# Part of a shared expert's work moved between the attention and the expert stage of a gated block with a mixture of experts

## The chip, the cores and the metric

The kernel is one launch on one core of a Trainium2 chip. The metric is the device time of that launch in microseconds (us). Five engines work side by side and meet only at semaphores: TensorE (PE, with PEld for its weight loads), VectorE (DVE), ScalarE (ACT), GpSimd (POOL) and SyncE (SP), which here only issues DMA transfers. Each engine runs its own instructions strictly in the order in which they are written, so an instruction that waits holds back all that stands behind it on that engine.

## What is computed

Sixteen batches of 128 tokens with 512 features go through cross attention and then through a mixture of experts; each part adds to its input through a gate.

```python
x = x + tanh(g_xattn) * attention(layernorm(x), ctx, pos, pos, Wq, Wkv, Wout, bout)   # 32 heads of 16, rotary
x = x + tanh(g_ffn)   * ffn(layernorm(x))

def ffn(x):                                     # 2048 tokens
    shared_out = silu_and_mul(x @ shared_w1.T) @ shared_w2.T       # inner width 704
    probs = softmax(x @ gate_w.T)                                   # 16 experts
    weights, selected = top_k(probs, 6)
    # each expert: silu_and_mul(x @ w1[e].T) @ w2[e].T, inner width 352, weighted, summed over the 6
    return moe_out + shared_out
```

All of it is float32; the large products are made from a high and a low part of each operand (x_hi, x_lo and w_hi, w_lo), three matmuls for one product.

## The kernel before

**Stage A, attention (`phase_a`).** A pipeline of five stages runs over the 16 batches: LOAD, PROJECT, ATTEND, TAIL, PLACE. In round r, stage k works on batch r - k, so there are 20 rounds: six written out, a loop, and four written out in which the stages run dry (rounds 16 to 19). A round has eight steps, u = 0 to 7. LOAD takes the statistics of the input (L868) and, at u = 7, scales it into `xn` (L875); PROJECT transposes `xn` on PE at u = 0 (L629) and makes q, k and v (L622), with POOL doing the rotary pairs (L429, L431); ATTEND makes scores (L647), their maxima on DVE (L902) and exponentials on ACT (L529); TAIL projects out (L734), adds the residual (L947), and scales it into `row` (L909) after POOL has made a reciprocal root by Newton steps (L436 to L447); PLACE transposes `row`, computes the gate, picks six experts for each token, and scatters the rows into an array in HBM sorted by expert (`expert_rows`, L459, POOL). On DVE, at u = 7, the order is `place`, then `row`, then `xn`. At the end of round 19 `block_table` builds on DVE a table that says for each block of 128 sorted rows which expert it belongs to; it is stored and loaded back by SP.

**Weights of the experts.** POOL splits each expert's weights into high and low parts (`split_w1` L205 and L209, `split_w2` L217 and L220) and loads the next ones (`load_after_split`). There are two places in SBUF (`SLOTS`), so the split of the weights after next waits until the expert that holds the place is done. The first two experts are split inside stage A, at the end of rounds 2 to 5 (`early_weights`): `split_w1` in rounds 2 and 4, `split_w2` in rounds 3 and 5.

**Between the stages** a block ends and another begins: all engines meet, then SP waits for the table, for all scattered rows and for the first padding rows, and only then loads the first rows of stage B.

**Stage B, experts (`phase_b`).** 143 steps: 111 steps (`BLOCKS`) of one routed block each, and then 32 for the shared expert, which is cut into two halves of width 352, two steps for each batch. Step i on PE is `down` of step i - 2 (L1413, 9 matmuls), `transpose_act` of step i - 1 (L1390, 3), `up` of step i (L1379, 24). On DVE a step turns the next tile (L1449), makes its low part `x_lo` (L1454), makes `a_lo` of step i - 1 (L1458) and `gated` of step i (L1470). SP loads each tile in four quarters (L1200) and the weights of its tokens (L1212), writes padding rows (L1191, L1192) during the first steps, and stores y.

**The end.** For each batch POOL gathers six rows of y for each token (L1301, six indirect DMAs). DVE adds them in `combine_rows` (L1477, 1536 elements wide) and `combine` (L1483 to L1486), and `finish` (L1493) adds the shared expert's result. The steps at which this happens are in `sum_at` and `finish_at`: one batch every two steps. POOL's two buffers let the gather of batch b start when `combine_rows` of batch b - 2 is done. The lines that set the order on DVE there:

```python
            if i is not None and i in finish_at and i != STEPS: finish(...)
            if starts_tile(i, 1): turn_x, meta, x_low
            if live(i, -1): a_low(*at(-1))
            if live(i, 0): gated(i, at)
            if i in sum_at: combine(sum_at[i])
            if i + 1 in sum_at: combine_rows(sum_at[i + 1])
```

## Time and profile before

| what | value |
|---|---|
| median of 3 runs | 1453.27 us (1451.62 to 1455.07) |
| the profiled execution | 1454.81 us, span 1452.9 us, mean granted PE clock 0.962 |
| PE busy | 1338.6 us, 92% of the span, 8414 matmuls |
| DVE, ACT, POOL busy | 764.0, 562.6, 698.3 us |
| PE's share of the chain that ended last | 74% |

The profile is of one execution. Times in it are counted from the first instruction; an engine's line number is that of the listing above. "Idle before" is the time in which the engine stood still just ahead of an instruction, with what released it. The granted clock is 1.0 at 2.4 GHz and 0.5 at 1.2 GHz.

### The profile page before, as it was taken

Reading aid. Unit: us, or ns where it says so; the run is one execution under the profiler, and the core shown is the slowest. Engines: PE = TensorE matmul, PEld = TensorE weight load, DVE = VectorE, ACT = ScalarE, POOL = GpSimd, SP = SyncE. Lnnn points to the kernel's source line nnn. Section 1 sums busy time; section 2 is a strip of 40 time slices with the busy share of each in tenths; the row PEclk is TensorE's granted clock in tenths of the full one; section 3 lists DMA queues with packets and bytes.
Section 4 is the critical chain, followed back from the end, with each engine's and each line's share of the span. In section 5 each row is a group of like instructions: output and inputs, shape, how many; then the busy total and the mean of one; then the engine's idle time right before and its main releaser. Section 6 shows DMA issues by size and latency. Waiting matters only on the chain.

```text
span 1452.9 us, 32739 instructions
## 1 busy us (share of the span) xinstructions
PE 1338.6 (92%) x8414; PEld 1144.2 (79%) x8415; DVE 764.0 (53%) x1554; ACT 562.6 (39%) x1366; POOL 698.3 (48%) x1135
## 2 busy tenths in 40 slices
PE   4897899989988639999999999999999999999998
PEld 2565666666666438999999999999999999898997
DVE  4467557667666443444444444444444443356666
ACT  3565566666666212333333333333233332211111
POOL 3556655555554333286554454545345500745553
PEclk8899899999999659999999999999999999999999
...
GB/s 194 30 93 79 138 98 134 77 89 142 77 103 102 81 186 142 140 148 148 119 141 108 148 148 143 145 140 148 148 145 143 113 115 88 117 161 213 196 206 145
DMA packets 146858, 190.04 MB, mean 131 GB/s; under 512 B 32531, under 2 KB 99604, under 8 KB 144116
## 3 DMA queue, kind: packets, MB, share of 16 engines
...
## 4 chain that ended last, share of the span: by engine, by line
PE 74%; DVE 7%; POOL 6%; issue 5%; ACT 4%; SPq 2%; POOLq 0%; DMA 0%; DVEq 0%; ACTq 0%
PE bank L1379 35%; PE bank L1413 19%; PE bank L622 4%; PE bank L629 3%; PE bank L1390 3%; PE bank L647 3%; PE bank L734 2%; ACT soft L529 2%; PE bank L661 2%; PE bank L678 1%; POOL w_lo L209 1%; DVE smax L902 1%; POOL newt L445 1%; DVE x L947 1%; POOL expert_rows L459 1%
## 5 line engine op out<-in xcount | busy, mean ns | idle before, releaser
L1379 PE MATMUL bank<-w_hi,x_hi 128*128 (+1 forms) x1144 | 289.2, 334 | 20.2 <-DVE x_lo L1454 18.2
L1379 PE MATMUL bank<-w_hi,x_lo 128*128 (+1 forms) x1144 | 276.9, 323 | 0.0
L1379 PE MATMUL bank<-w_lo,x_hi 128*128 (+1 forms) x1144 | 276.7, 323 | 0.0
L205 POOL CAST w_hi<-w_raw 128x352 fp32r<-128x352 f32 x144 | 69.0, 527 | 379.1 <-PE bank L1379 379.1
L1470 DVE SCALAR_TENSOR_TENSOR act<-silu,row_w,bank 128x352 f32<-128x352 f32 x111 | 64.4, 580 | 299.9 <-ACT silu L1328 299.4
L1328 ACT ACTIVATE silu<-bank 128x352 f32<-128x352 f32 x143 | 66.4, 464 | 400.8 <-PE bank L1379 400.8
L1379 PEld LDWEIGHTS bank<-w_hi,x_hi 128*128 128x128 f32 x1144 | 192.7, 189 | 20.7 <-issue 18.3
L1379 PEld LDWEIGHTS bank<-w_lo,x_hi 128*128 128x128 f32 x1144 | 199.8, 189 | 0.0
L1379 PEld LDWEIGHTS bank<-w_hi,x_lo 128*128 128x128 f32 x1144 | 199.3, 189 | 0.0
L1413 PE MATMUL bank<-w_hi,a_hi 128*128 (+3 forms) x429 | 171.4, 400 | 7.3 <-DVE a_lo L1458 7.0
L529 ACT ACTIVATE soft<-bank,smax 128x128 f32<-128x128 f32 x512 | 146.8, 379 | 80.1 <-DVE smax L902 80.1
L1317 ACT ACTIVATE x_hi<-x_t 128x512 fp32r<-128x512 f32 x127 | 80.2, 632 | 234.2 <-DVE x_t L1449 234.2
L1413 PE MATMUL bank<-w_hi,a_lo 128*128 (+3 forms) x429 | 169.7, 396 | 0.0
L1413 PE MATMUL bank<-w_lo,a_hi 128*128 (+3 forms) x429 | 169.5, 395 | 0.0
L1301 POOL DMA_INDIRECT gath<-y_rows,y_slots x96 | 96.9, 1010 | 90.7 <-DVE tree L1477 60.7
L209 POOL TENSOR_TENSOR w_lo<-w_raw,w_hi 128x352 fp32r<-128x352 f32 x144 | 137.5, 985 | 0.0
L1454 DVE TENSOR_TENSOR x_lo<-x_t,x_hi 128x512 fp32r<-128x512 f32 x127 | 113.7, 895 | 35.0 <-ACT x_hi L1317 29.8
L459 POOL DMA_INDIRECT expert_rows<-row,slots x96 | 94.7, 986 | 35.5 <-issue 33.1
L1449 DVE STREAM_TRANSPOSE x_t<-xr 128x512 f32<-128x512 f32 x127 | 89.8, 707 | 21.3 <-DMA xr<-expert_rows 21.0
L902 DVE TENSOR_REDUCE smax<-bank 128x4 f32<-128x512 f32 x128 | 84.8, 683 | 29.7 <-PE bank L647 28.7
L1413 PEld LDWEIGHTS bank<-w_hi,a_hi 128*128 128x128 f32 (+1 forms) x429 | 80.7, 188 | 23.7 <-DVE a_lo L1458 7.2
L1413 PEld LDWEIGHTS bank<-w_hi,a_lo 128*128 128x128 f32 (+1 forms) x429 | 80.9, 188 | 19.3
...
## 6 DMA issues: line engine op xcount, KB each, us to landing
...
y_rows<-y SPq DMA_DIRECT2D x111, 256.0 KB, 2.1
...
```

The lines of the kernel that those rows point to most:

```text
L205: nc.gpsimd.tensor_copy(w1_hi[d][half][:, s], w1_raw[:, d, halves[half]]).then_inc(w_hi_made, 1)
L209: nc.gpsimd.tensor_tensor(w1_lo[d][half][:, s], w1_raw[:, d, halves[half]], w1_hi[d][half][:, s].bitcast(F32), ALU.subtract).then_inc(w1_m ...
L459: g.indirect_dma_start(rows, bass.IndirectOffsetOnAxis(slots[j][:, k:k + 1], 0), row[j][:], None)\
L529: last = a.activation(soft[u % 2][:, h, :], bank[2 + u % 2][:, h * P:(h + 1) * P], ACT.Exp, bias=smax[u % 2][:, h:h + 1])
L902: v.tensor_reduce(smax[u % 2][:], s3, AX.X, ALU.max, negate=True).then_inc(smax_done, 1)
L1301: nc.gpsimd.indirect_dma_start(gath[b % 2][:, k, :], None, y_rows, bass.IndirectOffsetOnAxis(y_slots[:, b * 8 + k:b * 8 + k + 1], 0))\
L1317: a.activation(x_hi[j][:], x_t[:], ACT.Copy).then_inc(x_hi_done, 1)
L1328: a.activation(silu[j][:], g_bank[:, 0:WIDTH], ACT.Silu).then_inc(silu_done, 1)
L1379: last = nc.tensor.matmul(to[:, 0:WIDTH], xx[jt][:, d, :], w[d][half][:, cols], start=(d == 0 and xx is x_hi and w is w1_hi), stop=(d == D ...
L1413: last = nc.tensor.matmul(to[:], l[j][0:m, c, :], w[c][0:m, cols], start=(first and c == 0 and k == 0), stop=(final and c == 2 and k == 2))
L1449: v.transpose(x_t[:].rearrange("p c (i t) -> p i c t", i=4), xr[j][:].rearrange("p (i c e) -> p i c e", i=4, c=DC)).then_inc(x_turned, 1)
L1454: v.tensor_tensor(x_lo[j][:], x_t[:], x_hi[j][:].bitcast(F32), ALU.subtract).then_inc(x_lo_done, 1)
```

## The change

- **Half of the shared expert for batches 0 to 5 comes first.** Six steps (`EARLY = 6`) of its first half are numbered 0 to 5, the routed blocks are steps 6 to 116, and the shared expert's other 26 half steps follow. The number of steps stays 143. The result of an early step is added to x1 on DVE (`add_early`) and stored over x1 in HBM.
- **No block boundary.** Both stages' programs stand in one block. Early steps 0, 1 and 2 are laid by hand into rounds 17 to 19: their loads on SP, `turn_x` and `x_low` on DVE, `x_high` and `gate` on ACT, and on PE a quarter of `up` in each of u = 0 to 3 of round 18, the whole of step 1's at u = 6, and so on. Steps 3 to 5 follow `block_table`, and parts of the early steps stand between the links of that table's chain on DVE. SP waits for the table at step 3.
- **Weight splits.** The shared expert's first half is place 0, split in rounds 1 to 3 (half of `split_w1` in round 1, half in round 2, `split_w2` in round 3). The first routed expert's weights are split in rounds 17 and 18. The shared first half is loaded and split once more at the end, so there are 19 places (`PLACES`) for 18.
- **The input's scaling ahead of the row.** On DVE at u = 7, `xn` now stands ahead of `place` and `row`.
- **Order at the end.** `sum_at` puts a batch on every 1.4 steps from the fourth shared step on; on DVE the sums stand between `a_low` and `gated`; the first gather stands ahead of the last `split_w2`; five PSUM banks hold y for three.

The diff below is cut. Its pieces are, in order: the constants, POOL's splits in the early rounds, POOL's last rounds, PE's last rounds, DVE's round at u = 7, SP in stage B, POOL's last place, the steps of the sums, and DVE in a step of stage B.

```diff
+EARLY = 6
+ROUTED_END = EARLY + BLOCKS
+TILES = ROUTED_END + BATCHES
+PLACES = [EXPERTS, *range(EXPERTS), EXPERTS + 1, EXPERTS]
...
                     if r == 0:
                     pool.wait_ge(w_hi_done, 1)
                     load_w(nc.gpsimd, 0)
-                if r in (2, 4):
-                    split_w1(pool, r // 4)
-                if r in (3, 5):
-                    split_w2(pool, r // 4)
-                    load_after_split(pool, r // 4 + 1)
+                if r == 1:
+                    split_w1(pool, 0, range(0, 2))
+                if r == 2:
+                    split_w1(pool, 0, range(2, 4))
+                if r == 3:
+                    split_w2(pool, 0)
+                    load_after_split(pool, 1)
...
+                if last_round(at, ATTEND):
+                    pool.wait_ge(v_mm, BATCHES)
+                    clear_act()
+                    split_w1(pool, 1)
+                if last_round(at, TAIL):
+                    split_w2(pool, 1)
+                    load_after_split(pool, 2)
...
+                    if last_round(at, TAIL) and u < 4:
+                        up_part(0, u)
...
+                    if last_round(at, TAIL):
+                        if u == 4:
+                            transpose_act(0, 0, 0)
+                        if u == 6:
+                            for d in range(DC):
+                                up_part(1, d)
+                    if last_round(at, PLACE):
+                        if u == 0:
+                            down_part(2, 0)
+                            down_part(2, 1)
+                        if u == 1:
+                            down_part(2, 2)
+                            transpose_act(1, 1, 0)
+                            up_part(2, 0)
+                            up_part(2, 1)
+                        if u == 6:
+                            up_part(2, 2)
...
+                    if at(LOAD) and u == 7:
+                        load(u, *at(LOAD))
                     if at(PLACE) and u == 7:
                         place(*at(PLACE))
...
-                    if at(LOAD) and u == 7:
-                        load(u, *at(LOAD))
...
             def one_step(i, at):
+                if i == EARLY - 3:
+                    rows_complete()
...
+                    if place + 1 == len(PLACES):
+                        pool.wait_ge(slot_chain, 2 * EXPERTS - 1)
+                        for j in range(2):
+                            pool.wait_ge(y_out[j], 16 * (EARLY // 2 + (BLOCKS + 1 - j) // 2))
+                        gather(0)
...
+        sum_at = {ROUTED_END + 4 + math.ceil(1.4 * b): b for b in range(BATCHES)}
+        finish_at = {max(last_step[ROUTED_END + b] + 2, step + 1): b for step, b in sum_at.items()}
...
+                if shared and i - 1 in sum_at and sum_at[i - 1] < BATCHES - 1:
+                    combine(sum_at[i - 1])
+                if shared and i in sum_at:
+                    combine_rows(sum_at[i])
+                if shared and i in finish_at:
                     finish(finish_at[i])
                 if live(i, 0):
                     gated(i, at)
-                if i is not None and i in sum_at:
-                    combine(sum_at[i])
-                if i is not None and i + 1 in sum_at:
-                    combine_rows(sum_at[i + 1])
+                if i == STEPS - 1:
+                    combine(BATCHES - 1)
```

**Place 1: DVE at the end of a full round of stage A** (u = 6 and 7). Before, from the last two maxima of the scores to the input's scaling:

```order
L902 TENSOR_REDUCE smax<-bank 128x4 x2
L997 TENSOR_TENSOR slot_e<-bank,const 128x16
L999 TENSOR_TENSOR seen<-seen,mask 128x16
L1001 TENSOR_TENSOR pick_slot<-pick,slot_e 128x96
L1004 TENSOR_REDUCE slot_f<-pick_slot 128x6
L1007 CAST slots<-slot_f 128x8
L1008 COPY slots_all<-slot_f 128x8
L909 TENSOR_SCALAR row<-x,mean,rstd 128x4x4x32
L875 TENSOR_SCALAR xn<-x_sb,mean,rstd 128x512
```

After, the same stretch:

```order
L1009 TENSOR_REDUCE smax<-bank 128x4 x2
L982 TENSOR_SCALAR xn<-x_sb,mean,rstd 128x512
L1104 TENSOR_TENSOR slot_e<-bank,const 128x16
L1106 TENSOR_TENSOR seen<-seen,mask 128x16
L1108 TENSOR_TENSOR pick_slot<-pick,slot_e 128x96
L1111 TENSOR_REDUCE slot_f<-pick_slot 128x6
L1114 CAST slots<-slot_f 128x8
L1115 COPY slots_all<-slot_f 128x8
L1016 TENSOR_SCALAR row<-x,mean,rstd 128x4x4x32
```

`xn` has moved from behind `row` to ahead of the placing.

**Place 2: PE in round 18,** the last TAIL round, from the last values of attention (`soft_t`) on. Before, the attention's last transposes and the output projection (`at_hi`) follow at once:

```order
L678 MATMUL bank<-soft_t,v_one 17x128 x4
L629 MATMUL bank<-const,ot 128x128 x4
L629 MATMUL bank<-const,attn 128x128 x4
L734 MATMUL bank<-w_hi,at_hi 128x512
L734 MATMUL bank<-w_lo,at_hi 128x512
```

After (L1553 is `up` of the early step 0, a quarter at a time):

```order
L765 MATMUL bank<-soft_t,v_one 17x128 x4
L1553 MATMUL bank<-w_hi_0,x_hi 128x352
L1553 MATMUL bank<-w_hi_1,x_hi 128x352
L1553 MATMUL bank<-w_lo_0,x_hi 128x352
L1553 MATMUL bank<-w_lo_1,x_hi 128x352
L1553 MATMUL bank<-w_hi_0,x_lo 128x352
L1553 MATMUL bank<-w_hi_1,x_lo 128x352
L716 MATMUL bank<-const,ot 128x128 x4
```

Six expert matmuls have come in ahead of each of these waits.

**Place 3: DVE in the shared steps at the end.** Before, two steps of a pair:

```order
L1470 SCALAR_TENSOR_TENSOR act<-silu,tanh,bank 128x352
L1483 TENSOR_TENSOR tree<-tree 128x512
L1484 TENSOR_TENSOR tree<-tree,x_t 128x512
L1486 TENSOR_TENSOR comb<-tree 128x512
L1477 TENSOR_TENSOR tree<-gath 128x1536
L1493 TENSOR_TENSOR o_t<-bank,comb 128x512
L1458 TENSOR_TENSOR a_lo<-bank,a_hi 128x384
L1470 SCALAR_TENSOR_TENSOR act<-silu,tanh,bank 128x352
```

After, the seventh step behind the routed blocks, in which all three kinds of sum fall together:

```order
L1652 TENSOR_TENSOR a_lo<-bank,a_hi 128x384
L1648 TENSOR_TENSOR x_lo<-x_t,x_hi 128x512
L1682 TENSOR_TENSOR tree<-tree 128x512
L1683 TENSOR_TENSOR tree<-tree,x_t 128x512
L1685 TENSOR_TENSOR comb<-tree 128x512
L1676 TENSOR_TENSOR tree<-gath 128x1536
L1692 TENSOR_TENSOR o_t<-bank,comb 128x512
L1669 SCALAR_TENSOR_TENSOR act<-silu,tanh,bank 128x352
```

The sums have moved from behind `act` and ahead of `a_lo` to behind `a_lo` and ahead of `act`.

## Rows read from the trace of the kernel before

**Rows 1.** The page's 40 slices of the span, tenths busy and granted clock.

```profile
PE   4897899989988639999999999999999999999998
PEclk8899899999999659999999999999999999999999
```

**Rows 2.** Busy us (instructions) by stretch: PE, PEld, DVE, ACT, POOL; clock, DMA share, GB/s.

```profile
115.53:149.95 34.42, 26.63 (x205) 19.29 (x205) 24.33 (x50) 18.28 (x52) 25.17 (x51) 0.90 0.23 83
149.95:185.45 35.50, 29.23 (x205) 20.90 (x205) 19.61 (x50) 18.40 (x52) 21.82 (x44) 0.86 0.39 141
270.00:297.23 27.23, 25.13 (x206) 17.99 (x205) 18.64 (x50) 18.38 (x52) 14.45 (x35) 1.00 0.29 103
457.96:482.66 24.70, 19.28 (x168) 12.92 (x169) 14.67 (x41) 15.97 (x48) 8.82 (x21) 0.94 0.28 99
482.66:516.86 34.20, 18.80 (x78) 14.20 (x78) 13.26 (x52) 3.57 (x9) 14.76 (x25) 0.55 0.30 118
516.86:535.01 18.15, 0.00 (x0) 0.00 (x1) 6.92 (x30) 0.63 (x1) 7.02 (x9) 0.50 0.54 177
535.01:576.22 41.21, 37.59 (x196) 34.01 (x197) 15.05 (x28) 11.34 (x21) 10.17 (x15) 0.92 0.52 164
576.22:1232.86 656.64, 656.64 (x3781) 608.88 (x3781) 296.81 (x524) 205.98 (x421) 298.60 (x392) 1.00 0.45 135
1249.21:1447.36 198.15, 193.29 (x1093) 176.81 (x1092) 118.52 (x169) 36.91 (x76) 97.03 (x97) 1.00 0.63 184
```

**Rows 3.** Who waited for whom from 60 to 470: us in total, times, longest.

```profile
PE bank L629 <- DVE xn L875: 12.9, 13, 1.2
PE bank L629 <- POOL q_cos L431: 11.4, 2, 7.1
```

**Rows 4.** POOL by time in stage A: start, us, [idle before].

```profile
44.55 0.85 POOL L429 TENSOR_TENSOR q_cos<-q_cos,q_sin 128x256 f32<-128x256 f32 x1 [15.39 <-DVE q_sin L861]
...
125.99 7.12 POOL L209 TENSOR_TENSOR w_lo<-w_raw,w_hi 128x352 fp32r<-128x352 f32 x8
...
478.44 0.19 POOL L436 TENSOR_SCALAR neg_half<-mean 128x1 f32<-128x1 f32 x1 [12.26 <-DVE mean L952]
```

**Rows 5.** DVE at the end of round 15: start, us, [idle before].

```profile
432.28 0.55 DVE L909 TENSOR_SCALAR row<-x,mean,rstd 128x512 f32<-128x512 f32 x1 [2.38 <-POOL rstd L447]
432.74 0.54 DVE L875 TENSOR_SCALAR xn<-x_sb,mean,rstd 128x512 f32<-128x512 f32 x1
```

**Rows 6.** DVE from the last count to the first tile of stage B.

```profile
517.10 0.17 DVE L1022 TENSOR_TENSOR pad_at<-cnt,const 128x16 int32<-128x16 f32 x1
...
522.87 0.15 DVE L1055 TENSOR_SCALAR table_p<-tb 128x1 int32<-128x1 f32 x1
532.78 0.71 DVE L1449 STREAM_TRANSPOSE x_t<-xr 128x512 f32<-128x512 f32 x1 [9.76 <-DMA xr<-expert_rows]
```

**Rows 7.** PE by time: the first matmuls of `up` of step 112.

```profile
1243.56 0.59 PE L1379 MATMUL bank<-w_hi,x_hi 128*128 128x352 f32 x2 [2.04 <-POOL w_lo L209]
```

**Rows 8.** DVE in a shared step: the sums and what stands behind them.

```profile
1412.58 0.69 DVE L1486 TENSOR_TENSOR comb<-tree 128x512 f32<-128x512 f32 x1
1413.38 1.76 DVE L1477 TENSOR_TENSOR tree<-gath 128x1536 f32<-128x1536 f32 x1
1415.06 0.68 DVE L1493 TENSOR_TENSOR o_t<-bank,comb 128x512 f32<-128x512 f32 x1
```

**Rows 9.** All gathers: POOL's time for one issue, and to landing.

```profile
L1301 POOL DMA_INDIRECT gath<-y_rows,y_slots x96: 940/946/2291, 1249.5 to 1434.7; - x96
...
DMA to landing us min/median/max: 3.2/3.9/6.4
```

**Rows 10.** DVE beside POOL's splits: x_lo's ns min/median/max over 127, and one `prob`.

```profile
L1454 DVE TENSOR_TENSOR x_lo<-x_t,x_hi x127: 691/693/4192, 534.2 to 1428.9; 128x512 fp32r<-128x512 f32 x127
...
129.06 4.87 DVE L975 TENSOR_SCALAR prob<-gexp,grec 128x16 f32<-128x16 f32 x1
```

**Rows 11.** ACT's change from exponential to silu.

```profile
537.22 1.28 ACT L1328 ACT_TABLE_LOAD   x1
```

514 lines of the change are left out of this document (330 added, 184 removed).

## The prediction

> **What bounds the kernel now.** I read the page's slices first [rows 1]: PE is at nine tenths or more nearly everywhere, with one deep hole in slices 13 and 14, the hand-over from attention to experts, where its clock is also granted at half. So PE's order of work bounds the kernel, and gains can only come from places where PE stands still or runs at 1.2 GHz. The table by stretch gives these places their size [rows 2]. From 576.22 to 1232.86 PE does 105 routed steps without a gap: 656.64 / 105 = 6.25 us a step. I use that as the price of a step. A full attention round takes 27.23 us, of which PE is busy 25.1. Two early rounds take 34.42 and 35.50. From 457.96, where round 17 begins, to 576.22, where the sixth expert step's `up` has ended, 118.3 us pass. At the end 198.15 us hold 30 steps and the start of the last.
>
> The change leaves the number of expert steps at 143 and adds no matmul. I therefore sum what PE loses before and after in four places.
>
> **1. The weight splits in early rounds.** The two long rounds lose 34.42 + 35.50 - 2 x 27.23 = 15.5 us [rows 2]. PE waits 11.4 us of that, in two waits, the longest 7.1, for POOL's rotary pairs [rows 3]; POOL was in the splits behind a scatter, `w_lo` alone 7.12 us [rows 4]. The rest fits the granted clock, 0.90 and 0.86 in those rounds against 1.00 [rows 2]. After the change no split stands in rounds 4 and 5. Round 1 gets half a `split_w1`, about 5 us, where POOL idled 15.39 us [rows 4]; round 2 gets the other half where the whole was, round 3 keeps its `split_w2`. What hides them is that idle; without it they would cost what they cost now. I take **-15.5**; bounds -11.4 (only the waits go) and -18 (a remainder of low clock in the round after goes too).
>
> **2. `xn` ahead of `row`.** PE waited 12.9 us in 13 rounds for `xn` [rows 3], about 1 us each. On DVE `row` ended at 432.83, having waited for POOL's root, and `xn` only began at 432.74 [rows 5]. After, `xn` is made while DVE would idle (2.38 us before `row`), so it is hidden; PE has its 0.5 us of transposes to do and then meets the next wait, for `row`, which is ready at 432.88 against 432.78. About 0.1 of the 1.0 us stays, and DVE's next maximum moves forward by the 0.46 that `xn` took, not by 1.0. I take 0.8 for each of 13 rounds, **-10.5**; bounds 0 (the round closes on POOL's root and takes up the whole gain) and -13.
>
> **3. The hand-over.** Before: 118.3 us. After, in PE's order, with DVE and ACT followed along:
> - Round 17: 24.7 as before [rows 2], plus the tiles of the early steps on DVE (four operations of 0.7) of which perhaps half are hidden, plus their collisions with `split_w1`, which now stands on POOL ahead of the last-but-one root. That root idled 12.26 us [rows 4] and the split with its clearing takes 11.5, so POOL itself is just in time. I take 26.2.
> - From there to the end of `up` of step 5, PE has: attention's rest in rounds 18 and 19, about 9.7 us at full clock (18.80 us busy before at 0.55 [rows 2]); six `up`, four `down`, five transposes, 33.2 us. Sum 42.9. Waits: about 0.6 for the output projection, 1.8 for the last `row` (POOL's root is 3.7 us and only `up` of step 1 covers the chain from o to row), 0.3 small ones.
> - Step 6 needs the table and its rows. DVE's table chain took 5.8 us from the count [rows 6] and now also carries `gated`, `x_low`, `a_low` and `add_early`, 2.5 us and a short wait, so it ends about 9 us after the count. From its end to the first tile turned took 9.9 us before (522.87 to 532.78 [rows 6]); SP now has more padding rows ahead of it, and issues a store and an x1 load first. Set against steps 3 to 5, 18.7 us of PE work, tile 6 comes about 3 us late, and DVE stands before it with `a_low` and `gated` queued behind. I take 3.0.
> - The clock. Before, it fell near 480 and stayed at half for the hole (0.55, 0.50 [rows 2]). Step 112 shows what a short gap costs: a wait of 2.04 us [rows 7], then an `up` from 1243.56 to 1249.21, 5.65 us, where a step's 6.25 less `down` and transposes (2.43) leaves 3.82, so 1.8. I take that three times, once for round 18 and once behind each wait: 5.5 in all.
>
> After: 26.2 + 42.9 + 2.7 + 3.0 + 5.5 = 80.3; with 1.6 for what I can't see in a hand-made order, 81.9. **-36.4**; bounds -26 (round 18 at half clock all through, and a blocked DVE) and -43 (no loss of clock).
>
> **4. The end.** Before: `up` of step 112 waits 2 us for the last split and is 1.8 us long [rows 7]. 30 steps and the last `down`'s wait would be 30 x 6.25 + 3.5 = 191.0, and took 198.15 [rows 2], since `combine` and `combine_rows` stand ahead of `a_lo` in DVE's queue: 7.1. Together 10.9. After: the shared half that comes first is split while expert 15 runs, and the other one is needed six steps later, so the 3.8 goes. The sums now stand ahead of `act`. In a step with all three, `a_lo` ends 3.5 us after the step begins, then 0.6 (x_low) + 2.1 + 1.7 + 0.6 + 0.6 (act) (the sums by [rows 8]): 9.1, and PE wants `act` at 8.35 (one step and one `down`). Nine of the 26 steps have `combine` and `combine_rows` together. Four of them also make a tile: 0.75 late each; five do not: 0.15 each. That is 3.8, and the last `combine` now stands ahead of the last `a_lo`: 1.3. Together 5.1, so **-5.8**. The gathers: six issues of 0.95 with 0.3 between them are 7.5 us for each batch, and one every 8.75 us fits. Where two sums are only two steps apart there are 12.8 us for 7.5 + 3.9 to landing [rows 9], 1.1 to spare; at the longest landing, 6.4, three gathers are 1.4 late, and act with them. Bounds: +20 (below) and -9.
>
> **Sum.** 1454.8 (this execution) - 15.5 - 10.5 - 36.4 - 5.8 = 1386.6. The median of the three runs is 1.5 below this execution, so **1385**.
>
> **A rule against the change.** POOL's split in round 17 now runs beside DVE. In the profile `x_lo` takes 693 ns at the median and 4192 at the longest, and `prob` once took 4.87 us beside a split [rows 10]. The Trainium skill (SBUF — State Buffer, Who interferes with whom) says that a DVE instruction with two SBUF inputs, or in a two-port mode, and a GpSimd one that reads SBUF lock each other out for the whole instruction. By that rule each of about three such operations waits for one POOL instruction at most, under 1 us, and my 1.5 us for round 17 holds. The two long rows are longer than one POOL instruction, so the trace disagrees for them. By the rows, `prob` in round 17 could stand 5 us and all maxima behind it; this is rival B.
>
> The silu of the early steps alternates with the exponential of the gate: two more table loads on ACT at 1.28 [rows 11], both where ACT waits anyway. The Trainium skill (ScalarE: Activation LUTs, What ACT_TABLE_LOAD costs) gives 2.66 us for a switch with its drain; the trace shows 1.28 and no drain, and by the page too the loads would be hidden.
>
> **The rivals.**
> - **B, the hand-over is only half filled.** DVE blocked 5 us in round 17 (`prob` or `x_low`), and PE's clock at half through round 18, 9 us more: 1385 + 14 = 1399. For it: the long rows [rows 10], the clock before [rows 2]. Against: PE gets two `up` and more, 14 us of dense matmuls, in rounds 18 and 19.
> - **C, the reorder gives nothing,** because the round closes on POOL's root [rows 5]: 1385 + 10.5 = 1396.
> - **D, the early steps don't do what they should:** x1 or tile loads queued on SP behind padding rows hold `add_early`, DVE stands, and three steps run behind the table as before: 3 x 6.25 = 19, 1404.
> - **E, transfers bound the end.** Before, the stage moved 184 GB/s x 198 us = 36.5 MB with 0.63 of the DMA engines [rows 2]. Now the same bytes have the 155 us from the first gather on: 235 GB/s, which scales to 0.80. If the queues hold it to 207, the stage takes 176 us, 21 longer: 1406.
> - **F, slower than before.** The same mechanism with a price above all gains: the end would have to lose 68 us, so take 155 + 68 = 223 us for 36.5 MB, 164 GB/s. Below that the kernel is slower; at 160 it takes 228 us, 73 more: 1458. Against it: more than that was moved before with a third of the engines' time left.
> - **G, better:** no loss of clock in the hand-over, and early rounds gain their remainder: 1375.
>
> **How the numbers follow.** Forecast 0.58, B 0.13, C 0.07, D 0.04, E 0.08, G 0.07, F 0.02, and 0.01 for gains that cancel. The range for 8 in 10 goes from 1370 to 1406: it takes in the forecast with its own spread (1375 to 1396), B, C, D and half of G, and leaves out most of E, F and what lies below 1370. About 0.2%, 3 us, is what a measurement of this kernel tells from no change. Faster by more: 0.97. Within: 0.01. Slower: 0.02.
>
> **What would show it.** Step 1: no wait of PE for q_cos, xn to xn in rounds 5 and 6 near 26.5. Step 2: rounds of about 26.4 us and no wait for xn; if they stay at 27.2, C. Step 3: from the first scores of round 17 to the end of the sixth expert `up`, 82 us; a wait of PE at round 19's row near 1.8 and at step 6 near 3; a long `prob` or `x_lo` in round 17 means B; waits for `add_early`'s x1 mean D. Step 4: no wait for `w_lo` after the routed blocks; waits for `act` below 1 us in the shared steps; DVE waiting for gathers, and landings over 6 us, mean E. The forecast is wrong if PE's time per step moves from 6.25, since 143 steps carry it.

## The result, and the profile after

The changed kernel took **1404.12 us** (median of 4 runs, 1401.31 to 1406.85), the kernel before 1452.44 in the same runs: ratio 0.9668, 95% interval 0.964 to 0.9696. Forecast were 1385, with 1370 to 1406 as the range. The direction was right and the time lies in the range, but 17 to 19 us of the forecast gain of 68 are missing.

The profiled execution spans 1402.3 us, against 1452.9 before. First the page's slices of the changed kernel, to be read beside [rows 1]:

```profile
PE   4899999999998988999999999999999999999998
PEclk8899999999997899999999999999999999999999
```

The hole of slices 13 and 14, counted from 0 (busy 6 and 3, clock 6 and 5), has shrunk: slices 12, 14 and 15 stand at 8, and the clock at 7 and 8 in slices 12 and 13. Then the stretches that answer to [rows 2]; the columns are those of that group:

```profile
112.30:137.87 25.57, 25.11 (x207) 18.13 (x205) 18.70 (x50) 18.42 (x52) 14.81 (x34) 1.00 0.32 111
137.87:163.93 26.06, 25.11 (x206) 18.06 (x205) 18.34 (x49) 18.42 (x52) 14.57 (x34) 1.00 0.32 109
216.84:243.16 26.32, 25.32 (x206) 18.04 (x204) 18.72 (x49) 18.54 (x52) 14.79 (x35) 1.00 0.30 106
426.72:458.42 31.70, 26.23 (x168) 16.99 (x169) 22.36 (x46) 17.15 (x50) 20.66 (x39) 0.72 0.44 143
458.42:508.18 49.76, 47.30 (x273) 41.54 (x273) 30.78 (x97) 13.61 (x25) 29.25 (x41) 0.94 0.67 240
508.18:556.63 48.45, 36.60 (x182) 32.85 (x182) 17.39 (x32) 9.85 (x20) 18.83 (x25) 0.86 0.61 186
556.63:1182.98 626.35, 626.35 (x3602) 582.41 (x3602) 283.42 (x500) 196.53 (x401) 309.63 (x406) 1.00 0.45 137
1182.98:1402.30 219.32, 208.51 (x1173) 189.92 (x1171) 132.59 (x193) 47.44 (x95) 118.84 (x118) 0.99 0.62 187
```

The first two rows are rounds 5 and 6: 25.57 and 26.06 us where they were 34.42 and 35.50. The third is a full round, 26.32 against 27.23. The fourth is round 17, which became longer, 31.70 against 24.70, at a clock of 0.72. The fifth ends with the sixth expert `up`. The sixth is what I had not foreseen: 48.45 us in which PE is busy for 36.60, right behind the hand-over. The seventh has no gap, as before.

These edges cut both executions at the same places of PE's program:

| stretch | before | after | moved | forecast |
|---|---|---|---|---|
| start to the first scores of round 17 | 457.96 | 426.72 | -31.2 | -26.0 |
| from there to the end of the sixth `up` | 118.3 | 81.5 | -36.8 | -36.4, with |
| the next 105 steps | 656.6 | 674.8 | +18.2 | the line above |
| the last 32 steps | 220.0 | 219.3 | -0.7 | -5.8 |
| span | 1452.9 | 1402.3 | -50.6 | -68.2 |

The forecast's term for the hand-over held a wait at step 6 and its low clock too, and these fall into the third row. So the hand-over is worth 36.8 - 18.2 = 18.6 us, not 36.4. PE's waits over 2 us from round 17 on, in the changed kernel by time (start, us, engine, line, operation, [idle before, and who ended it]):

```profile
450.62 0.63 PE L748 MATMUL bank<-const,soft 128*128 128x128 f32 x2 [3.47 <-ACT soft L595]
...
514.57 0.80 PE L1598 MATMUL bank<-w_hi,a_hi 128*128 128x512 f32 x1 [6.38 <-DVE a_lo L1652]
...
547.53 0.79 PE L1598 MATMUL bank<-w_hi,a_hi 128*128 x1 [5.47 <-DVE a_lo L1652]
...
1272.92 0.47 PE L1598 MATMUL bank<-w_hi,a_hi 128*128 128x512 f32 x1 [2.40 <-DVE o_t L1692]
```

Four waits, and each became a question for the experiments. For the first, DVE's row beside POOL's in round 17:

```profile
440.74 6.09 DVE L1648 TENSOR_TENSOR x_lo<-x_t,x_hi 128x512 fp32r<-128x512 f32 x1
```

```profile
439.10 7.18 POOL L214 TENSOR_TENSOR w_lo<-w_raw,w_hi 128x352 fp32r<-128x352 f32 x8
```

`x_lo` of step 0 takes 6.09 us instead of 0.69, beside POOL's split of expert 0, and everything behind it on DVE, the maxima among it, is late. For the second and third, DVE's turnings of tiles 6 and 10, and under them what SP issues before tile 6 and tile 10 (start, us, line, transfer, count):

```profile
511.54 0.71 DVE L1643 STREAM_TRANSPOSE x_t<-xr 128x512 f32<-128x512 f32 x1 [8.48 <-DMA xr<-expert_rows]
...
544.47 0.71 DVE L1643 STREAM_TRANSPOSE x_t<-xr 128x512 f32<-128x512 f32 x1 [7.75 <-DMA xr<-expert_rows]
```

```profile
490.17 10.34 SPq L417 DMA_DIRECT2D expert_rows<-v_one  x8
500.56 0.35 SPq L463 DMA_DIRECT2D block_table<-table_p  x1
502.14 1.43 SPq L417 DMA_DIRECT2D expert_rows<-v_one  x2
503.62 0.33 SPq L466 DMA_DIRECT2D table<-block_table  x1
...
507.99 1.90 SPq L1338 DMA_DIRECT2D xr<-expert_rows  x4
...
531.64 0.85 SPq L1377 DMA_DIRECT2D expert_rows<-pad_row  x2
532.54 0.44 SPq L1356 DMA_DIRECT2D x_rows<-y  x1
533.78 2.24 SPq L1338 DMA_DIRECT2D xr<-expert_rows  x4
```

DVE's last link of the table began at 496.82, but SP is in its eight padding rows until 500.5 and stores the table only then. Tile 10's quarters are issued at 533.78 and turned at 544.47. Just ahead of them stand two dump rows and a store on SP, and on POOL's queue 2.1 MB of weights:

```profile
531.77 0.60 POOL L199 DMA_DIRECT2D w_raw<-in_w  x1 [0.58 <-POOL w_lo L225]
```

### The profile page after: what moved, and what is told of

Its sections match the earlier page's. It is cut to its first block, busy times and chain, and to the rows that moved or that the text cites. A ratio compares the mean times of both kernels' runs of the same rounds, so it can differ in the third digit from the quotient of the medians.

```text
span 1402.3 us, 33052 instructions
## 1 busy us (share of the span) xinstructions
PE 1331.2 (95%) x8414; PEld 1138.1 (81%) x8415; DVE 770.2 (55%) x1572; ACT 571.2 (41%) x1374; POOL 728.0 (52%) x1160
## 3 DMA queue, kind: packets, MB, share of 16 engines
q1 hardware_dynamic: 130292, 104.03, 24.8%
## 4 chain that ended last, share of the span: by engine, by line
PE 75%; DVE 8%; issue 5%; ACT 4%; SPq 3%; POOL 2%; DMA 1%; POOLq 0%; DVEq 0%; ACTq 0%
PE bank L1553 35%; PE bank L1598 19%; PE bank L709 5%; PE bank L1565 3%; PE bank L734 3%; PE bank L716 3%; PE bank L748 2%; ACT soft L595 2%; PE bank L821 2%; PE bank L765 1%; DVE smax L1009 1%; DVE x L1054 1%; DVE attn L1048 1%; DVE stats L1057 1%; ACT at_hi L620 1%
## 5 line engine op out<-in xcount | busy, mean ns | idle before, releaser
L1553 PE MATMUL bank<-w_hi,x_hi 128*128 (+1 forms) x1144 | 289.6, 334 | 0.0
L1553 PE MATMUL bank<-w_hi,x_lo 128*128 (+1 forms) x1144 | 277.3, 323 | 0.0
L1553 PE MATMUL bank<-w_lo,x_hi 128*128 (+1 forms) x1144 | 277.0, 323 | 0.0
L210 POOL CAST w_hi<-w_raw 128x352 fp32r<-128x352 f32 x152 | 72.9, 529 | 370.7 <-PE bank L1553 370.7
L1553 PEld LDWEIGHTS bank<-w_lo,x_hi 128*128 128x128 f32 x1144 | 199.2, 188 | 0.0
L1553 PEld LDWEIGHTS bank<-w_hi,x_lo 128*128 128x128 f32 x1144 | 199.0, 188 | 0.0
L1553 PEld LDWEIGHTS bank<-w_hi,x_hi 128*128 128x128 f32 x1144 | 192.4, 189 | 0.4 <-issue 0.4
L1484 ACT ACTIVATE x_hi<-x_t 128x512 fp32r<-128x512 f32 x133 | 84.0, 632 | 195.6 <-DVE x_t L1643 195.6
L214 POOL TENSOR_TENSOR w_lo<-w_raw,w_hi 128x352 fp32r<-128x352 f32 x152 | 146.1, 992 | 0.0
L1648 DVE TENSOR_TENSOR x_lo<-x_t,x_hi 128x512 fp32r<-128x512 f32 x133 | 125.1, 941 | 28.4 <-ACT x_hi L1484 23.2
L1426 POOL DMA_INDIRECT gath<-y_rows,y_slots x96 | 101.2, 1055 | 47.9 <-issue 26.5
L1652 DVE TENSOR_TENSOR a_lo<-bank,a_hi 128x384 fp32r<-128x384 f32 x143 | 79.3, 555 | 51.7 <-ACT a_hi L1489 50.7
L1643 DVE STREAM_TRANSPOSE x_t<-xr 128x512 f32<-128x512 f32 x133 | 93.7, 704 | 22.3 <-DMA xr<-expert_rows 22.3
```

The source lines that it names most:

```text
L210: nc.gpsimd.tensor_copy(w1_hi[d][half][:, s], w1_raw[:, d, halves[half]]).then_inc(w_hi_made, 1)
L214: nc.gpsimd.tensor_tensor(w1_lo[d][half][:, s], w1_raw[:, d, halves[half]], w1_hi[d][half][:, s].bitcast(F32), ALU.subtract).then_inc(w1_m ...
L1426: nc.gpsimd.indirect_dma_start(gath[b % 2][:, k, :], None, y_rows, bass.IndirectOffsetOnAxis(y_slots[:, b * 8 + k:b * 8 + k + 1], 0))\
L1484: a.activation(x_hi[j][:], x_t[:], ACT.Copy).then_inc(x_hi_done, 1)
L1553: last = nc.tensor.matmul(to[:, 0:WIDTH], xx[jt][:, d, :], w[d][half][:, cols], start=(d == 0 and xx is x_hi and w is w1_hi), stop=(d == D ...
L1643: v.transpose(x_t[:].rearrange("p c (i t) -> p i c t", i=4), xr[j][:].rearrange("p (i c e) -> p i c e", i=4, c=DC)).then_inc(x_turned, 1)
```

## The experiments

Stage lengths read within one trace are steadier than medians here: the code up to round 17 is the same in the changed kernel and in e3 to e12, and yet round 17 begins between 425.6 and 430.5 us in their profiled executions. The first rounds make that spread. So each run is told by its time and by four lengths of its trace: (a) the first scores of round 17 to the end of the sixth `up`, (b) from there to the start of `up` 10, (c) to the start of `up` 123, (d) to the end.

| run | median us | ratio to before (95%) | a | b | c | d |
|---|---|---|---|---|---|---|
| changed kernel | 1404.12 | 0.9668 (0.964 to 0.9696) | 81.5 | 43.8 | 708.1 | 142.2 |
| e1 | 1414.82 | 0.9722 (0.9698 to 0.9746) | 81.3 | 43.8 | 707.6 | 142.1 |
| e2 | 1418.49 | 0.9754 (0.9734 to 0.9774) | 74.7 | 43.1 | 709.7 | 140.6 |
| e3 | 1403.17 | 0.9653 (0.9631 to 0.9674) | 80.5 | 42.8 | 707.6 | 142.0 |
| e4 | 1409.48 | 0.9685 (0.965 to 0.9719) | 81.3 | 43.5 | 708.4 | 144.8 |
| e5 | 1404.54 | 0.9677 (0.9657 to 0.9696) | 79.0 | 43.5 | 710.3 | 140.6 |
| e6 | 1398.3 | 0.9615 (0.9584 to 0.9645) | 81.3 | 33.1 | 711.6 | 142.0 |
| e7 | 1398.75 | 0.9633 (0.9613 to 0.9654) | 81.7 | 35.9 | 709.5 | 142.1 |
| e8 | 1399.8 | 0.9656 (0.9628 to 0.9684) | 81.3 | 42.1 | 708.2 | 138.7 |
| e9 | 1399.86 | 0.9632 (0.9612 to 0.9652) | 76.7 | 41.1 | 707.6 | 142.1 |
| e10 | 1385.89 | 0.9536 (0.9517 to 0.9556) | 76.7 | 31.8 | 711.4 | 140.4 |
| e11 | 1396.94 | 0.9617 (0.9594 to 0.9639) | 76.6 | 29.0 | 721.6 | 137.4 |
| e12 | 1387.2 | 0.9527 (0.9506 to 0.9547) | 78.1 | 29.0 | 715.9 | 140.2 |

e1 to e4, e5 to e8 and e9 to e11 ran together on one chip each. The medians of different groups are therefore best compared by their ratios. Put on a before of 1452.4 us, the ratios set the runs against the changed kernel at +7.8 us (e1), +12.5 (e2), -2.2 (e3), +2.5 (e4), +1.3 (e5), -7.7 (e6), -5.1 (e7), -1.7 (e8), -5.2 (e9), -19.2 (e10), -7.4 (e11) and -20.5 (e12). Only e1, e2, e10, e11 and e12 have intervals apart from the changed kernel's. For the others the time alone decides nothing, and the readings below rest on the waits and lengths of one trace each. In the traces whose code is unchanged there, a is 81.3 to 81.7 and d 140.6 to 142.1.

### e1: `xn` behind `row` again

The two lines move from ahead of `place` and `normalised_row` to the end of DVE's round, where the kernel before has them:

```
-                    if at(LOAD) and u == 7:
-                        load(u, *at(LOAD))
...
+                    if at(LOAD) and u == 7:
+                        load(u, *at(LOAD))
```

> The changed kernel with its second part alone undone: xn is made behind row again. Stage A gained 31.2 us where 26.0 were forecast, and this run splits that. Theory 1 (the extra 5 us belongs to the splits and xn is worth the 10.5 I gave it): 1404 + 10.5 = 1414 to 1416, rounds back from 26.4 to about 27.2, PE waits about 1 us for xn in 13 rounds. Theory 2 (xn is worth more, about 1 us in every one of 16 rounds, since PE's wait for xn also put the next maximum late): 1419 to 1421. Rival C of the prediction (the reorder gives nothing): 1404.

10.7 us slower than the changed kernel by the medians, 7.8 by the ratios, and from round 6 on the rounds are 27.2 to 27.3 us apart again. The wait of [rows 3] is back (who waited for whom, 60 to 440 us: total, times, longest):

```profile
PE bank L716 <- DVE xn L982: 13.1, 13, 1.3
```

In the changed kernel's trace, from 60 to 427, that wait is gone, and 2.9 us in 10 waits for `row` stand in its place:

```profile
PE bank L716 <- DVE row L1016: 2.9, 10, 0.4
```

13.1 - 2.9 = 10.2, which speaks for theory 1; the time (7.8 to 10.7 us) excludes rival C and theory 2, but doesn't fix the size closer than that. Part 2 is worth about what the forecast gave it, so the surplus of stage A should be the splits'; e2 asks that.

### e2: the splits in rounds 2 to 5 again, none in round 17

```
-                if r == 1:
-                    split_w1(pool, 0, range(0, 2))
-                if r == 2:
-                    split_w1(pool, 0, range(2, 4))
-                if r == 3:
-                    split_w2(pool, 0)
-                    load_after_split(pool, 1)
+                if r in (2, 4):
+                    split_w1(pool, r // 4)
+                if r in (3, 5):
+                    split_w2(pool, r // 4)
+                    load_after_split(pool, r // 4 + 1)
...
                     clear_act()
-                    split_w1(pool, 1)
-                if last_round(at, TAIL):
-                    split_w2(pool, 1)
-                    load_after_split(pool, 2)
```

> The changed kernel with all weight splits back in rounds 2 to 5 (whole ones), and none in rounds 17 and 18. It undoes step 1 and at the same time takes the splits away from beside x_low. Theory 1 (step 1 is worth 15.5, and the 6.09 us x_lo of round 17 with the 3.47 us wait of PE behind it comes from the split beside it): rounds 4 and 5 go back to about 34 and 35 us, round 17 shrinks from 31.7 to about 27.5; together +15.5 - 4 = 1415 to 1416. Rival (x_lo is long for another reason): x_lo of step 0 stays at about 6 us without a split beside it, and the time is 1404 + 15.5 = 1419.5 or more.

14.4 us slower by the medians (12.5 by the ratios), near both numbers, so the time doesn't separate them; the trace does, and shows that both effects are larger than I had them. Rounds 5 and 6, and PE's wait in them:

```profile
112.69:147.13 34.44, 26.45 (x206) 19.31 (x205) 24.90 (x50) 18.32 (x53) 25.16 (x51) 0.90 0.24 83
147.13:182.00 34.87, 29.36 (x207) 21.20 (x206) 19.43 (x51) 18.44 (x53) 21.83 (x43) 0.85 0.40 144
```

```profile
PE bank L710 <- POOL q_cos L488: 12.6, 2, 7.6
```

They are 34.44 + 34.87 - 25.57 - 26.06 = 17.7 us longer, and rounds 2 to 4 add some: the last `xn` is made at 419.78 against 398.43, so stage A loses 21.3. And length a is 74.7 instead of 81.5: without a split beside it, `x_lo` takes its normal time:

```profile
462.42 0.68 DVE L1642 TENSOR_TENSOR x_lo<-x_t,x_hi 128x512 fp32r<-128x512 f32 x1
```

Of the 21.3, 17.7 stand in rounds 5 and 6 and 2.4 in round 3 (27.2 us between two `xn` against 24.8; in e3 to e12, with the new splits, 24.8 to 25.7); the other 1.3 is no more than the first rounds differ between runs. So the splits' new place in rounds 17 and 18 costs 6.8 us, and the old one cost 19 to 20.

Is it the blocked operation that makes round 17 long, or the low clock in it? The clock fell before the block: in the changed kernel it stood at 0.50 from 433.8 to 443.8, and `x_lo` began at 440.74. Round 17 in e2, and in e8, whose code is the changed kernel's up to the end of the routed steps:

```profile
448.07:474.58 26.51, 21.44 (x168) 14.45 (x169) 16.95 (x46) 17.04 (x50) 10.02 (x23) 0.86 0.53 171
```

```profile
427.20:458.93 31.73, 21.96 (x168) 14.31 (x168) 23.36 (x46) 17.11 (x50) 20.68 (x39) 0.85 0.43 143
```

At nearly the same clock, 0.86 and 0.85, the round takes 26.51 us without a split beside it and 31.73 with one, where `x_lo` took 7.11; in the changed kernel the clock was 0.72 and the round no longer, 31.70. So the block sets its length, 5.2 of the 6.8 us, and the clock does not; the other 1.6 stand in rounds 18 and 19.

### e3 and e5: the blocked operation moved about

e3, on DVE (and ACT's `x_high` of step 1 from u=5 to u=7; the `x_low(1, 1, 0)` taken out here comes back at u=0 of round 18, which the cut leaves out):

```
                         if u == 1:
                             turn_x(0, 0, 0)
-                        if u == 3:
-                            x_low(0, 0, 0)
-                        if u == 4:
-                            turn_x(1, 1, 0)
                         if u == 6:
-                            x_low(1, 1, 0)
+                            x_low(0, 0, 0)
+                            turn_x(1, 1, 0)
```

> The changed kernel with x_low of step 0 moved from u=3 of round 17 to u=6, behind POOL's split of expert 0 (439 to 446 us), and step 1's turn_x, x_high and x_low moved after it. Nothing else is moved. Theory 1 (DVE's 6.09 us x_lo beside the split is what PE waits 3.47 us for, and starts the low clock): x_lo 0.7 us, PE's wait gone, round 17 about 27.5 instead of 31.7, 1404 - 4 = 1400. Rival 1 (any two-input DVE operation beside the split is blocked, x_lo was only the one that was there): another one takes 4 to 6 us, 1404. Rival 2 (the clock falls anyway when the rounds' projections end): the wait goes but the clock is at half from 433 on as before, 1402.

e5, on top of e3:

```
-                    if at(PLACE) and u in (0, 1, 3):
-                        gate(u, *at(PLACE), gate_ch)
+                    if at(PLACE) and u in ((0, 1, 4) if last_round(at, ATTEND) else (0, 1, 3)):
+                        gate(min(u, 3), *at(PLACE), gate_ch)
```

> The kernel of e3 (x_low behind u=6 in round 17), and besides the prob part of batch 13's gate is moved from u=3 to behind the maxima of u=4 in that round. e3 showed prob at 5.55 us in the place where x_lo took 6.09 before, both ending with POOL's run of w_lo. Theory 1 (the first DVE operation of this kind stands until POOL's run of eight w_lo ends at about 447; placed behind the maxima it costs nothing): the maxima of u=4 end before 447, PE's wait of 2.6 to 3.5 us for soft shrinks to under 1.5, prob still shows as long but short of its end at 447; 1403 - 3 = 1400. Rival (the maxima read PSUM through the same port and are blocked as well, once prob is out of the way): the maxima take over 3 us and the time stays 1403.

DVE and POOL in round 17 of e3, then of e5:

```profile
440.84 0.68 DVE L1009 TENSOR_REDUCE smax<-bank 128x4 f32<-128x512 f32 x1
441.43 0.15 DVE L1080 RECIPROCAL grec<-gsum 128x1 f32<-128x1 f32 x1
441.62 5.55 DVE L1082 TENSOR_SCALAR prob<-gexp,grec 128x16 f32<-128x16 f32 x1
```

```profile
439.98 7.16 POOL L214 TENSOR_TENSOR w_lo<-w_raw,w_hi 128x352 fp32r<-128x352 f32 x8
```

```profile
445.80 0.69 DVE L1009 TENSOR_REDUCE smax<-bank 128x4 f32<-128x512 f32 x1 [3.00 <-PE bank L734]
446.40 0.15 DVE L1080 RECIPROCAL grec<-gsum 128x1 f32<-128x1 f32 x1
446.59 2.31 DVE L1082 TENSOR_SCALAR prob<-gexp,grec 128x16 f32<-128x16 f32 x1
```

```profile
441.68 7.19 POOL L214 TENSOR_TENSOR w_lo<-w_raw,w_hi 128x352 fp32r<-128x352 f32 x8
```

In e3 rival 1 holds: `prob`, an operation on 16 columns that takes 0.23 us in the changed kernel, stands 5.55 us in the place of `x_lo`, and ends at 447.17; POOL's run of eight ends at 447.14. In e5 it starts at 446.59 and ends at 448.90, the run at 448.87. So what is blocked stands until POOL's whole run is over, however long it began before, and the maxima, which read PSUM, pass beside it at 0.68 and 0.69. Against theory 1 of e5, the time did not move (1404.54): PE's wait behind the maxima stayed (3.27 us), since `prob` and the chain behind it, 4.0 us together, now stand ahead of the next maxima. Round 17 took 30.78 us in e3 and 29.01 in e5, where e2 has 26.51. The block is shown; moving the blocked operation took away about half of its price at most.

### e9: the run cut in two

```
                     clear_act()
-                    split_w1(pool, 1)
+                    split_w1(pool, 1, range(0, 2))
+                    pool.wait_ge(mask_done, BATCHES - 2)
+                    split_w1(pool, 1, range(2, 4))
```

> The changed kernel with POOL's split of expert 0 in round 17 cut in two: chunks 0 and 1 as before, chunks 2 and 3 only when DVE has made batch 13's mask (the end of the chain in which prob stands). e2, without the split in that round, was 7.5 us shorter from the last xn to the end; e3 and e5 moved the blocked operation about and gained nothing, since the chain behind it stayed late. Theory 1 (the wait is the length of POOL's unbroken run of w_lo, here 7.2 us, and half a run costs under half): x_lo or prob at most 2.5 us, the maxima of u=5 come 3 us sooner, PE's wait for soft under 1.5 us, 1404 - 4 = 1400. Rival (the second half now blocks the residual's two-input operations, and POOL's root comes as late as it does now): PE's wait for soft shrinks but row comes later, 1404.

4.3 us faster than the changed kernel by the medians, 5.2 by the ratios, and length a is 76.7, near the 74.7 of e2 without any split there. DVE's `x_lo`, and PE's waits in the second half of round 17:

```profile
443.94 1.38 DVE L1650 TENSOR_TENSOR x_lo<-x_t,x_hi 128x512 fp32r<-128x512 f32 x1
```

```profile
450.93 1.13 PE L736 MATMUL bank<-k_t,q_t 32*128 32x256 f32 x8 [0.50 <-ACT soft L597]
454.01 0.65 PE L750 MATMUL bank<-const,soft 128*128 128x128 f32 x4 [0.47 <-ACT soft L597]
457.59 1.11 PE L718 MATMUL bank<-const,row 128*128 128x128 f32 x4 [2.58 <-DVE row L1018]
```

The 1.38 us are still a block, of a shorter run: the first half's four `w_lo` end at 444.78 and `x_lo` at 445.32. Theory 1 holds, with a part of the rival: the 3.47 became 0.50, and `row` now waits 2.58 for POOL's root, which stands behind the second half.

### e6 and e7: the two waits behind the table

e6, on SP: `first_pads(range(0, 5))` ahead of the table's store, `range(5, 7)` between store and load, `range(7, 8)` behind the load. The other padding rows, first ahead of a step's tile load, now behind it:

```
-                if i is not None and EARLY - 2 <= i < EARLY + 1:
...
-                    pads(range(10 + 2 * k, 12 + 2 * k))
...
+                if i is not None and EARLY <= i < EARLY + 4:
...
+                    pads(range(8 + 2 * (i - EARLY), 10 + 2 * (i - EARLY)))
```

with the dump rows in step 10, behind the load, and the loop beginning two steps later.

> The changed kernel with SP's order around the table altered: five padding rows, the table's store, two, the table's load, one; the other eight and the dump rows behind the tile loads of steps 6 to 10 instead of ahead of them in steps 4 to 7. Theory 1 (SP's queue makes tile 6 late, and its 6.7 us of issues a step hold tiles 7 to 10): table loaded about 4.5 us sooner, PE's wait of 6.38 at step 6 falls to about 2, the 5.47 wait at down(8) falls below 2, with their low clock together 1404 - 9 = 1395. Rival 1 (only the first is SP's doing; tile 10 is late because of 2.1 MB of weights on the DMA engines at 532 to 544): the first wait shrinks, the second stays at 4 to 6 us, 1404 - 5 = 1399. Rival 2 (tile 6 waits for the table chain of DVE): both stay, 1404.

e7, on POOL:

```
+                    if place == 2:
+                        pool.wait_ge(y_mm, EARLY + 5)
                     if place + 1 < len(PLACES):
                         load_after_split(pool, place + 1)
```

> The changed kernel with one more wait on POOL: the weights of expert 2 are loaded only after the down of step 10, some 25 us later. Theory 1 of the second stall (tile 10's quarters, issued at 533.8, land at 544.4 because the 2.1 MB of weights issued at 531.8 to 533.7 fill the DMA engines): the wait of 5.47 at down(8) goes, and the 3.2 us of low clock behind it, 1404 - 8.5 = 1395.5. Rival (SP is late by itself, pads and dump rows): the wait stays above 3, 1402 to 1404.

Both take the second wait away, and e6 more than half of the first: lengths b are 33.1 and 35.9 against 43.8. PE and DVE at step 6 in e6:

```profile
514.41 0.79 PE L1599 MATMUL bank<-w_hi,a_hi 128*128 128x512 f32 x1 [2.89 <-DVE a_lo L1653]
```

```profile
511.74 0.71 DVE L1644 STREAM_TRANSPOSE x_t<-xr 128x512 f32<-128x512 f32 x1 [5.35 <-DMA xr<-expert_rows]
```

In e7 SP issued tile 10's quarters at 534.71, 0.9 us later than in the changed kernel, and without 2.1 MB of weights around them the tile was turned 4.2 us after that, not 10.7:

```profile
538.92 0.71 DVE L1645 STREAM_TRANSPOSE x_t<-xr 128x512 f32<-128x512 f32 x1 [0.92 <-DMA xr<-expert_rows]
```

In e6 tile 10's quarters were issued at 529.20, ahead of those weights (532.44), and DVE turned the tile without a wait. So the 5.47 us wait needs two things at once: a tile asked for late, and the weights of expert 2 on the DMA engines at that moment. Either taken away ends it. Its size is not steady: in e8, whose code is the same there, it was 3.39 us. The tile was late mainly because tile 6 was; SP needed 6.7 us a step from tile 6 to tile 9, register work included, where a step is 6.26, and 5.7 from there to tile 10, so its issues kept it late more than they added to it. The first wait is SP's order for 3.5 of its 6.38 us. The median moved by 5.8 in e6 and 5.4 in e7 (7.7 and 5.1 by the ratios), less than the 10.8 and 7.9 of length b; e6 gives 3.4 back in length c, see below, and began round 17 3.5 us later than the changed kernel's execution.

### e4 and e8: the order of the sums

e4:

```
-                if shared and i in sum_at:
-                    combine_rows(sum_at[i])
                 if shared and i in finish_at:
                     finish(finish_at[i])
                 if live(i, 0):
                     gated(i, at)
+                if shared and i in sum_at:
+                    combine_rows(sum_at[i])
```

> The changed kernel with the order of DVE in the last 26 steps changed: a_low, x_low, combine, finish, gated, and only then combine_rows (1.76 us), which falls into DVE's idle time between act and the next a_lo (1.85 us). The last stage lost 9.0 us up to the last up and 1.85 more at the last down. Theory 1 (the late act and the late finish of a full step are what PE waits for): nearly all of the 9.0 goes, 1404 - 8 = 1396. Rival (rows of y arrive late; DVE would wait for gathers once they are asked for earlier or the sums are off the path, and the transfers bound the stage): 1404 within 2, with waits of DVE for gath in the trace.

e8 exchanges only the first two: `finish` ahead of `combine_rows`.

> The changed kernel with finish (o_t) ahead of combine_rows (1.76 us) in the last 26 steps; nothing else. Theory 1 (the 2.40 us wait at 1272.9, which the trace gives to o_t, is the down of step 123 waiting for the bank that finish of batch 1 reads, and its half clock costs 1.8 more): the wait falls to about 0.7, the other full steps stay as they are, 1404 - 3.3 = 1400.7. Rival (act behind it would be as late anyway): down comes on time and the transposes of act wait the same; at most 0.5 gained, 1403.6.

PE in e8 at the place of the changed kernel's 2.40 us wait, then a full step in the changed kernel, then the last `down` in e4:

```profile
1269.86 0.47 PE L1598 MATMUL bank<-w_hi,a_hi 128*128 128x512 f32 x1 [0.73 <-DVE o_t L1692]
```

```profile
1303.43 0.55 PE L1565 MATMUL bank<-const,act 128*128 128x128 f32 x3 [1.26 <-DVE act L1669]
```

```profile
1400.02 0.80 PE L1598 MATMUL bank<-w_hi,a_hi 128*128 128x512 f32 x1 [3.59 <-DVE a_lo L1652]
```

e8 confirms the cause in its theory 1: the wait falls by 1.67 us, to the 0.73 expected, and the `down` takes 2.31 instead of 3.81 us, so that length d falls by 3.4 (3.3 were expected). Only the 1.67 is surely the edit's: in e2 and e5, where the wait stayed, the clock did not fall either and d is 140.6, 1.9 above e8; by the ratios e8 is 1.7 us faster. The wait was for a bank: `down` of batch 6 writes where batch 1's sum is still to be read. e4 is refuted: d grew by 2.7. Behind `act` the 1.76 us of `combine_rows` and the 0.7 of a turning are more than DVE's idle 1.85, so in the full steps `a_lo` came 1.5 us late and PE still waited 0.56 to 1.45, once behind rows of y that had not landed (DVE waited 1.92); and PE waited longer for the last `a_lo`, 3.59 against 1.85. The wait for `o_t` at this place stayed as well, 2.28 us, though `finish` stands ahead of `combine_rows` in e4 too: `combine_rows` of the step before had pushed all of DVE's work back.

### e10, e11, e12: put together

e10 is e9, e6 and e8 in one kernel.

> The changed kernel with e9's halves, e6's order on SP and e8's finish first together. By the medians of those runs against the before of their own call, set beside the changed kernel's ratio of 0.9668: e6 -7.7, e8 -1.7 (its trace -3.4), e9 as it comes out (-4 forecast). If they add up, ratio about 0.9545, 1387 for a before of 1452. Rival (the places hide one another: with the last split earlier the table chain is the bound, as e6's first wait of 2.89 shows): 1391 or more.

e11 adds e7 and two further edits: at step 5, `a_low`, `add_early` and `gated` ahead of `turn_x` (ACT: `a_high` and `gate` ahead of `x_high`); and `gather(1)` ahead of the last w2 split with the sums at steps 3, 4, 6, 8, 9, 10, 12, 13, 15, 16, 17, 19, 20, 22, 23 and 25 behind the routed ones.

> e10, and besides: the weights of expert 2 loaded after the down of step 10 (e7); at step 5 a_low, add_early and gated ahead of the turning of tile 6, so that PE's down(4) does not wait for the table; the gather of batch 1 ahead of the last w2 split, and the sums of batches 0 to 2 one step sooner. Theory 1: the wait behind up(5) (2.89 in e6) goes, as 2.4 us of PE's work come ahead of it, with its low clock 3 to 4 us; the o_t wait of 0.73 and one late act of the end go, 1 to 2 us: e10 - 5, about 1382. Rival (at step 5 PE only waits one instruction later; gathers come too late for the earlier sums): e10 within 2.

e12 is e10 with the edit of step 5 alone:

```
+                if i == EARLY - 1:
+                    a_low(*at(-1))
+                    add_early(*at(-2))
+                    gated(i, at)
+                    turn_x(*tile(i, at, 1))
+                    meta(*at(1))
+                    x_low(*tile(i, at, 1))
+                    return
```

> e10 with one of the three further edits of e11: at step 5 a_low, add_early and gated stand ahead of the turning of tile 6 on DVE, and a_high and gate ahead of x_high on ACT. In e11 this left 0.93 and 0.33 us of waits at step 6 where e10 has 2.89 and half clock behind it; e11 lost its time at the two other edits (4.86 at down(11) behind the late weights, 4.00 at the first sums). Theory 1: those two are out, so e10 - 3 to 4: 1382 to 1383, no wait over 1 us between steps 5 and 12. Rival (the loss of e11 belongs to the reorder as well, since add_early's store and the next loads on SP shift): e10 or slower, 1386 and above.

In e10 the mends add up: 1385.89 at a ratio of 0.9536 (0.9545 was expected), some 1.4% faster than the changed kernel (0.9668), and 4.6% faster than the kernel before. e11's theory is refuted: it is 11 us slower than e10, where 5 faster were expected. e12 is at 0.9527 with an interval that overlaps e10's: its waits between steps 5 and 12 went as expected, but the 3 to 4 us are not seen in its time. The rest of the three runs tells how gains are given back. e11's edit of step 5 does what it should (0.93 and 0.33 us of waits at step 6 for 2.89), but the late weights now meet a tile three steps on, and the earlier sums run beside the last split (there DVE's four sums of 0.68, 0.68, 0.69 and 1.76 us took 1.09, 1.77, 1.66 and 2.03); PE in e11:

```profile
562.72 0.79 PE L1609 MATMUL bank<-w_hi,a_hi 128*128 x1 [4.86 <-DVE a_lo L1663]
...
1247.36 0.90 PE L1576 MATMUL bank<-const,act 128*128 128x128 f32 x3 [4.00 <-DVE act L1680]
```

And in e12, where both edits are out, length c is 715.9 against 708.1. DVE, POOL and PE at one of four such places:

```profile
763.65 4.86 DVE L1656 TENSOR_TENSOR x_lo<-x_t,x_hi 128x512 fp32r<-128x512 f32 x1
```

```profile
759.01 7.29 POOL L214 TENSOR_TENSOR w_lo<-w_raw,w_hi 128x352 fp32r<-128x352 f32 x8
766.25 1.72 POOL L222 CAST w_hi<-w_raw 128x512 fp32r<-128x512 f32 x3
```

```profile
769.12 0.50 PE L1606 MATMUL bank<-w_hi,a_hi 128*128 x1 [1.63 <-DVE a_lo L1660]
```

The block of round 17 also occurs in the routed steps, where the changed kernel had it in none, e2, e5 and e7 in one, e6 and e10 in two and e12 in four: 4.77 to 4.86 us on DVE each, 1.63 to 1.75 of wait on PE. Four waits of 1.63 to 1.73 us are 6.6 of the 7.8 us by which e12's length c is longer; the clock stayed at 1.00 there. Whether an edit or the single execution deals these blocks is not shown, as each run has one trace. For the execution speaks that e12's profiled one, at 1393.38 us, was the longest of five with the same code (from 1382.33).

## Why the prediction was right, and where it fell short

**What bounds it, and the price of a step:** right. A step is still 6.26 us and PE has no wait between 556.63 and 1182.98.

**The sum as a whole.** The forecast was -68.2 for the profiled execution and became -50.6. The hand-over gave 17.8 less than forecast, outside its own bounds of -26 to -43, and the end 5.1 less; stage A gave 5.2 more, some 4 of it by e2 the splits', which lie outside their bound of -18. That these partly cancel is luck, and it helped the time into the range.

**1, the weight splits:** forecast -15.5, -18 at the most; e2 shows 19 to 20 in stage A. The two waits and the low clock of rounds 5 and 6 are 17.7 of it, near the upper bound. What I left out is round 3: with the whole splits of rounds 2 and 3 it was 1.5 to 2.4 us longer than with their new form.

**2, `xn` ahead of `row`:** forecast -10.5, e1 10.7 by the medians and 7.8 by the ratios. The mechanism is in the trace too: the wait for `xn` went, a wait for `row` of 0.3 us in 10 rounds took its place. Rival C is refuted.

**3, the hand-over:** forecast -36.4, became -18.6. The failed terms, one by one:
- *Round 17, 26.2:* took 31.7. This is the first half of rival B: a DVE operation blocked for 5 us. I had weighed the rows ([rows 10]) against the rule of the Trainium skill (SBUF — State Buffer, Who interferes with whom), by which a DVE operation with two SBUF inputs and a GpSimd one that reads SBUF lock each other out for one instruction, and took the side of the rule with 1.5 us for all collisions. The trace disagrees with it for these operations: 6.09 us is over six of POOL's instructions of 0.9. The row of `prob` at 4.87 was the better guide. e2 prices it at 5.2 in round 17 (26.51 us there, close to the 26.2), e9 takes back 4.6 of that. The second half of rival B, the low clock through round 18, came only in part: the clock was 0.72 in round 17 and 0.94 from 458.42 to 508.18. My sign of 82 us up to the sixth `up` was met, at 81.5, by luck: those 82 held the wait at step 6 and its clock, 4.8 us that fall behind this edge, and round 17 ran over by 5.5.
- *Step 6, 3.0:* took 6.38. The forecast named SP's padding rows ahead and gave them no price. Eight of them take 10.34 us, and the table's store stood 3.6 us behind the end of the chain that made it. e6 took back 3.5.
- *Behind step 6, nothing:* took 5.47 and the clock with it. The sum stopped at the first late tile. It did not ask how late SP asks for the tiles behind tile 6 (6.7 us of its time a step, for 6.26), nor when POOL, whose split ends there, loads the next weights. From the end of the sixth `up` to `up` 10 a steady kernel takes 2.3 + 4 x 6.26 = 27.3 us; it took 43.8, e12 29.0.
- *The clock, 5.5:* about right in its kind, too small in number, since there were more waits. A `down` behind 6.38 or 5.47 us of wait took 4.2 us where 2.25 is normal (3.7 behind 6.38 in e2), the one behind 2.40 us 3.81; but the same wait of 2.40 in e2 and e6 was followed by 2.30 and 2.32 us. So a wait of this length sometimes costs the clock and sometimes not.
- *The table loads:* two more came on ACT, 1.28 us each, as forecast. Behind the first of the early steps (467.82) the silu began at once, at 469.12, so no drain shows here either.

**4, the end:** forecast -5.8, was -0.7. The 3.8 us at step 112 went as forecast: PE has no wait there. The full steps were to cost 3.8 and cost 9.0 up to the last `up`. Of that 4.2 is one place, the bank that `finish` of batch 1 sets free behind `combine_rows` (e8), a dependency that the sum had not looked at: it asked only when `act` is ready. The other steps with a tile were 0.94 late where I had 0.75, two in a row 1.48, and those without a tile 0.34 where I had 0.15. The last `down` waited 1.85. Gathers and transfers did not bound it: landing was 3.3 to 6.4 us, DVE never waited for rows of y, so rivals E and F are refuted. D's wait for x1 at the early steps is not there, and those steps don't run behind the table; what D said of tile loads behind padding rows on SP did happen, but one step later, at step 6.

The nearest rivals by their time were right in number, E at 1406 wrong in mechanism and D at 1404 in all but that queue; B at 1399 names only a part of what happened.
